# Paged attention in two halves of the heads: one run of 32 tiles instead of two of 16, with the second half's weights prepared in between

## Chip, cores, metric

One core of one Trainium2 chip. The metric is the device time of one execution in microseconds (us), the median of the runs. All times in this text are of that core.

## What is computed

`x` is (64, 32, 512) in fp32. First a quantised linear layer with a low-rank part is added to it, then an attention layer:

```python
x = x + _L0_cond_ref(x, weight, scale_log, codebook, lora_A, lora_B)   # x @ w_eff.T
# attention: B, S, HID = 64, 32, 512; D, HQ, HK = 128, 32, 8; 64 pages of 32 keys, 16 pages a batch
q = rope(rmsnorm(x @ Wq.T, q_norm_w)); k = rope(rmsnorm(x @ Wk.T, k_norm_w)); v = x @ Wv.T
kc, vc = k_cache[block_table], v_cache[block_table]            # 512 old keys a batch
probs = softmax(where(valid, q @ concat(kc, k).T / sqrt(D), -1e30))    # 4 query heads a key head
x = x + (probs @ concat(vc, v)) @ Wo.T
```

## The kernel before, in words

fp32 products are made of three fp16 products (high x high, high x low, low x high), so every operand lies in SBUF as a high and a low part, and most of the data that is turned or loaded is split by ScalarE (high) and VectorE (low).

The setup, once: constants and the effective weight of the first layer (a loop over 63 thresholds: VectorE L554 compares, ScalarE L470 and L471 make diagonals, TensorE L437 sums), while the key pages are turned and split and written to DRAM (`keys_transposed`) and the value pages are split (ScalarE L466, GpSimd L621) and written too. GpSimd starts this stage with the page numbers (L608 to L610: cast, clamp, cast), from which it makes the row numbers of the value gathers (`rows`, L616) and the positions (L617), which VectorE needs for the angles of the rope table (L510). Then `x + layer 1` is made and written transposed to DRAM in 16 tiles of 128 rows (`x1_transposed`).

The heads are done in two halves (4 key heads, 16 query heads), since the weights of one half fill SBUF: `Wt` (projections, six groups of 512 columns: K, four of Q, V) and `WoT` (output, four groups). `with nc.Fori(0, HALVES)` runs three blocks for each half, with a barrier and a clearing of the semaphores after each:

- `tile_block(..., prep=True)`: the weights of this half are loaded to a stage of 1 MB (`load_stage`), turned by TensorE (`turn_weights`, L1052, 40 pieces of four fp32 transposes), split by ScalarE L1157 and VectorE L1268 into `Wt` and `WoT`; in between runs the projection of tile 0.
- `tile_block(..., attn=True)`: 16 tiles of 4 batches. A tile has 16 slots, one for each pair of batch and key head (a unit). In slot s every engine runs, in an order written out by hand: scores of unit s (TensorE L964, L967; VectorE `maxima` L1209; ScalarE `exps` L1110), the turning of the probabilities of unit s - 2 (TensorE L975, ScalarE `probs_high` L1104, VectorE `probs_low` L1214), the values of unit s - 3 (TensorE L998, L1000) and the results of unit s - 4 (ScalarE L1119, VectorE L1227). `TILE_PLAN` spreads over the slots of a tile the projection for the next tile (TensorE L1018, norm on ScalarE and GpSimd, rotation on VectorE L1247 and L1248 at slots 3, 5, 8, 10, 12, turning through the PSUM bank `TRp`, L1028) and the output projection of the tile before (L1039, 48 matmuls in nine parts). Tile 15 has no projection, tile 0 no output projection. After the last slot the pipeline is flushed.
- `tile_block(..., wo=[0])`: the output projection of the last tile, with the first two weight loads for the next half.

SP's queue goes batch by batch: when the maxima of a batch are done, the mask for two batches on, when its scores are done, the 16 pages of keys for three batches on (three buffers); behind these the other loads of the tile, by the place b of the batch in its tile: y (b 0), the new values to DRAM (b 1) and back (b 2), xT for three tiles on (b 2), the rope table for three tiles on and the store of y (b 3). xT and the rope table have two buffers each. The values of a batch are gathered by GpSimd's indirect DMAs (L767), four of 128 rows a batch, one batch ahead, on a queue of their own.

## Time and profile before

| | before |
|---|---|
| median of 3 runs | 2333.78 us (2333.56 to 2333.95) |
| profiled execution | 2333.03 us |
| its span, first to last instruction | 2331.4 us |
| TensorE matmul busy | 2190.5 us, 94% |
| VectorE, ScalarE, GpSimd busy | 1745.9 (75%), 1472.9 (63%), 1245.9 us (53%) |
| mean granted TensorE clock | 0.978 |
| data moved | 419.55 MB, mean 180 GB/s |

The mean of TensorE's share hides its stages: the setup (to 275 us), the preparation of half 1 (to 335), a run of 16 tiles, the stretch between the halves (from some 1270 to 1363), the second run, and the end. Read it stage by stage.

### The profile page before, as it was taken

How to read it: one execution, taken by the hardware profiler on the slowest of the kernel's cores; microseconds unless marked ns; L12 is line 12 of the kernel's file. 1: busy time of each engine (PE TensorE's matmuls, PEld its weight loads, DVE VectorE, ACT ScalarE, POOL GpSimd, SP SyncE). 2: the span in 40 equal slices, each digit the busy share in tenths (PEclk: the TensorE clock that was granted, in tenths of full speed). 3: DMA queues.
4: the chain of work that ended last, by engine and by line, in shares of the span. 5: the costliest groups of instructions: out<-in, count | busy, mean ns of one | idle time of the engine just before them, and what ended most of it. 6: DMA issues, size and time to landing. Idle time of an engine off the chain costs nothing. (4 is left out here: it accounts for less than half of the span.)

```text
span 2331.4 us, 61112 instructions
## 1 busy us (share of the span) xinstructions
PE 2190.5 (94%) x18068; PEld 1425.2 (61%) x18068; DVE 1745.9 (75%) x3942; ACT 1472.9 (63%) x4968; POOL 1245.9 (53%) x2066
## 2 busy tenths in 40 slices
PE   5886789999999999999998789999999999999997
PEld 2443456666666666666665456666666666666664
DVE  6995468777777777777777377777777777777774
ACT  2542367676666666676765466667677666666663
POOL 4330036666666666666664146666666666666562
PEclk9997889999999999999999899999999999999999
DMA  2785666566666666566654665666566666666563
GB/s 100 241 297 161 220 203 178 175 177 177 183 176 185 181 177 180 177 179 178 174 174 130 204 184 171 182 178 177 177 178 180 184 184 179 178 179 177 169 185 108
DMA packets 445186, 419.55 MB, mean 180 GB/s; under 512 B 51615, under 2 KB 371437, under 8 KB 444846
## 3 DMA queue, kind: packets, MB, share of 16 engines
q1 hardware_dynamic: 399726, 277.08, 40.5%
q0 software_dynamic: 40960, 134.25, 19.1%
q10 hardware_dynamic: 4160, 4.19, 0.5%
q8 instruction: 152, 2.49, 0.4%
q14 instruction: 188, 1.54, 0.2%
HBM read 369.12 MB, written 46.21 MB: 178 GB/s over the span
## 5 line engine op out<-in xcount | busy, mean ns | idle before, releaser
L767 POOL DMA_INDIRECT pages<-values_split,rows_s x512 | 516.8, 1009 | 133.3 <-issue 119.8
L1018 PE MATMUL PR<-Wt,xT 128*128 128x512 f16 x2304 | 559.6, 381 | 3.7 <-DVE Wt L1268 3.7
L1104 ACT ACTIVATE pts<-PTp 128x512 f16<-128x512 f32 x512 | 306.7, 599 | 341.4 <-PE PTp L975 277.4
L998 PEld LDWEIGHTS Op<-pts,pages 128*128 128x128 f16 x6144 | 383.3, 98 | 137.6 <-DVE OT L1227 19.3
L998 PE MATMUL Op<-pts,pages 128*128 128x128 f16 x6144 | 427.3, 219 | 17.5 <-DVE OT L1227 12.1
L964 PE MATMUL Sp<-pages,qT 128*128 128x512 f16 x1536 | 417.0, 380 | 7.1 <-PEq L178 6.6
L1110 ACT ACTIVATE masked<-masked,small 128x544 f32<-128x544 f32 x512 | 380.4, 743 | 58.8 <-DVE small L1209 43.7
L1214 DVE TENSOR_TENSOR pts<-PTp,pts 128x512 f16<-128x512 f32 x512 | 351.8, 687 | 86.9 <-ACT pts L1104 50.8
L1209 DVE CUSTOM_DVE_ANT_0 masked<-Sp,mask 128x544 f32<-128x544 f32 x512 | 369.9, 722 | 51.2 <-PE Sp L967 30.8
L1039 PE MATMUL WOp<-WoT,OT 128*128 128x512 f16 x1536 | 379.7, 382 | 9.8 <-PEq L178 9.8
L1018 PEld LDWEIGHTS PR<-Wt,xT 128*128 128x128 f16 x2304 | 225.9, 98 | 200.1 <-issue 9.9
L1227 DVE TENSOR_TENSOR OT<-Op,OT 128x128 f16<-128x128 f32 x512 | 148.3, 290 | 240.2 <-ACT p L1098 153.6
L975 PE MATMUL PTp<-ident,masked 128*128 128x128 f32 x2048 | 325.4, 282 | 1.9 <-DVE pts L1214 1.8
L1220 DVE TENSOR_SCALAR masked<-masked,small 128x544 f32<-128x544 f32 x512 | 291.8, 570 | 18.1
L1325 POOL CAST n<-masked 128x64 f16<-128x64 f32 x512 | 122.0, 238 | 337.8 <-DVE masked L1220 201.5
L1119 ACT ACTIVATE OT<-Op 128x128 f16<-128x128 f32 x512 | 143.6, 281 | 189.3 <-PE Op L980 152.8
L1039 PEld LDWEIGHTS WOp<-WoT,OT 128*128 128x128 f16 x1536 | 146.0, 98 | 131.8 <-issue 15.3
L975 PEld LDWEIGHTS PTp<-ident,masked 128*128 128x128 f32 x2048 | 214.5, 140 | 2.7 <-issue 2.3
L1318 POOL TENSOR_TENSOR qr<-qr,rs_ 128x512 f32<-128x512 f32 x160 | 203.0, 1269 | 6.5 <-DVE rs_ L1248 6.5
L964 PEld LDWEIGHTS Sp<-pages,qT 128*128 128x128 f16 x1536 | 140.1, 98 | 100.9 <-issue 10.6
L1313 POOL TENSOR_TENSOR small<-small 128x4 f32<-128x4 f32 x160 | 184.4, 1153 | 13.3
L967 PEld LDWEIGHTS Sp<-kTn,qT 128*128 128x128 f16 x1536 | 113.8, 97 | 121.8 <-issue 1.7
(196 smaller groups left out, 3070.8 us busy)
## 6 DMA issues: line engine op xcount, KB each, us to landing
pages<-keys_transposed SPq DMA_DIRECT2D x2048, 64.0 KB
mask<-mask_rows SPq DMA_DIRECT2D x128, 128.0 KB
v<-new_values SPq DMA_DIRECT2D x96, 128.0 KB
pages<-in_L_cond_Wq SPq DMA_DIRECT2D x9, 1024.0 KB, 7.3
keys_transposed<-pages SPq DMA_DIRECT2D x32, 256.0 KB, 3.0
values_split<-pages SPq DMA_DIRECT2D x16, 512.0 KB, 3.5
xT<-x_transposed SPq DMA_DIRECT2D x32, 256.0 KB
pages<-values_split,rows_s POOLq DMA_INDIRECT x512
```

What stands on the lines that cost most here:

```text
L767: nc.gpsimd.indirect_dma_start(out=vS[:, n % 2, c, :, :].rearrange("p l n -> p (l n)"), out_offset=None, in_=v_d, in_offset=bass.IndirectO ...
L964: nc.tensor.matmul(Sp[:, 512:1024].rearrange("p (a n) -> p a n", a=NPP), qT[:, tt, ql, q0:q0 + P], kT[n % KBUFS][:, :, h, kl, :], start=(k ...
L975: m = nc.tensor.transpose(PTp[:, c * P:(c + 1) * P], masked[:, u % 3, S + c * P:S + (c + 1) * P], ident[:, :])
L998: nc.tensor.matmul(o, vS[:, par, c, low, h * D:(h + 1) * D], pts[:, u % 2, part, c * P:(c + 1) * P], start=(k == 0), stop=False)
L1018: m = nc.tensor.matmul(bank(k), xb[:, c, xl, :], Wp[:, c, wl, GROUP_COL[k]:GROUP_COL[k] + HID], start=(i == 0), stop=(i == NPASS - 1))
L1039: m = nc.tensor.matmul(WOp[:, :], OT[:, 1 - tt, hq, ol, :], WoT[:, hq, wl, :], start=(hq == 0 and ol == 0 and wl == 0), stop=(hq == QHH - ...
L1104: nc.scalar.activation(pts[:, u % 2, 0, :], PTp[:, :], ACT.Copy).then_inc(G.pt_hi, 1)
L1110: nc.scalar.activation(masked[:, u % 3, :], masked[:, u % 3, :], ACT.Exp, bias=nmax[u % 2], scale=-1.0, accum_out=psum_row[u % 2]).then_in ...
L1209: V.tensor_tensor_reduce(out=masked[:, u % 3, :], in0=Sp[:, 512 - S:1024], in1=mask[:, par, :], scale=-SCALE, scalar=BIG, op0=ALU.add, op1 ...
L1214: V.tensor_tensor(pts[:, u % 2, 1, :], PTp[:, :], pts[:, u % 2, 0, :], ALU.subtract).then_inc(G.pt_lo, 1)
L1220: V.tensor_scalar(masked[:, u % 3, :], masked[:, u % 3, :], rinv[u % 2], None, ALU.mult).then_inc(G.norm_done, 1)
L1318: nc.gpsimd.tensor_tensor(qr[:, m_ % 2, :], qr[:, m_ % 2, :], rs_[:, :], ALU.add).then_inc(G.rope_done, 1)
```

## The change

The loop over the halves is gone. The preparation block runs once, for half 1; then one attention block runs 32 tiles (`ALL_TILES`). Tile 15 now has the projection for tile 16, and tile 16 the output projection of tile 15; the output projection of tile 31 is done by key head inside the flush. Half 2's weights are made in 40 pieces: `load_piece` brings 128 columns of a group (512 B a row) to `wsrc` (two buffers), `turn_piece` turns them through `TRp` at the end of slots 1, 8 and 13 of tiles 0 to 13 (without the first and the last of these 42), ScalarE and VectorE split them into `wdst` one slot later, and `store_piece` writes them to DRAM. The six projection groups are loaded to `Wt` in tile 14, each once its last use there is done, and the four output groups to `WoT` in tile 16. To make room, xT and the rope table have one buffer instead of two, `squares` writes its unused result to `qn` (`sq` is gone), and the copy `rows_s` of the row numbers is gone. GpSimd makes a second list of page numbers, raised by 64, in the setup, with three more instructions.

```diff
+PIECES = (GROUPS + KVH) * 4
+PIECE_SLOTS = [UPT * t + sl for t in range(TILES - 2) for sl in (1, 8, 13)][1:PIECES + 1]
...
                 link(Q.tensor_scalar(btf, btf, float(PAGES - 1), 0.0, ALU.min, ALU.max))
                 Q.tensor_copy(bt_raw, btf).then_inc(G.pages_bounded, 1)
                 g.wait_ge(G.pages_bounded, 1)
+                link(Q.tensor_scalar(btf, btf, 1.0, float(PAGES), ALU.mult, ALU.add))
+                Q.tensor_copy(bt_next, btf).then_inc(G.pages_bounded, 1)
+                g.wait_ge(G.pages_bounded, 2)
+                link(Q.tensor_scalar(btf, btf, 1.0, -float(PAGES), ALU.mult, ALU.add))
...
+        def load_piece(sp, p):
+            s, j = divmod(p, 4)
+            sp.dma_start(wsrc[:, p % 2, :].rearrange("p (c n) -> p c n", c=4), weight_source(1, s)[:, :, j * P:(j + 1) * P]).then_inc(wsrc_loaded[p % 2], 16)
+        def store_piece(sp, p):
+            sp.dma_start(wd_d[p // 4, :, p % 4, :], wdst[:, :, :].rearrange("p l n -> p (l n)")).then_inc(G.w_stored, 16)
...
@@ SP, prep block
                         sp.wait_ge(v5_loaded[0], 3 * 16)
+                        sp.wait_ge(G.proj_done, GROUPS)
+                        load_xT(sp, 1)
+                        sp.wait_ge(G.xT_loaded, 32)
@@ SP, attention block, past = batch - KBUFS, ti, b = divmod(past, BPT)
                             if past >= 0:
                                 sp.wait_ge(G.max_done, KVH * (past + 1))
                                 load_mask(sp, past + 2)
+                                while pieces < PIECES and PIECE_SLOTS[pieces] + 2 <= KVH * (past + 1):
+                                    sp.wait_ge(G.w_lo, pieces + 1)
+                                    store_piece(sp, pieces)
+                                    if pieces + 2 < PIECES:
+                                        load_piece(sp, pieces + 2)
+                                    pieces += 1
+                                if b == 2 and ti + 2 < NT:
+                                    sp.wait_ge(G.proj_done, GROUPS * (ti + 1))
+                                    load_xT(sp, ti + 2)
                                 sp.wait_ge(G.qk_done, KVH * (past + 1))
-                            load_pages(sp, half, numbers, batch % KBUFS)
+                            if batch < NB:
+                                load_pages(sp, numbers, batch % KBUFS)
...
                             if b == 3:
-                                if ti + 3 < TILES:
+                                if ti + 2 < NT:
                                     sp.wait_ge(G.rope_part, len(NORMED) * (ti + 1))
-                                    load_table(sp, ti + 3)
+                                    load_table(sp, ti + 2)
                                 if ti in wo:
                                     store_y(wo.index(ti))
+                            if ti == TILES - 2:
+                                sp.wait_ge(G.w_stored, 16 * PIECES)
+                                for k in ((0, 1), (2, 3), (4, 5), ())[b]:
+                                    sp.wait_ge(G.proj_done, GROUPS * ti + k + 1)
+                                    load_group(sp, k)
+                            if ti == TILES:
+                                for g, parts in (((), (), ((0, 4),), ((1, 6), (2, 7), (3, 9)))[b]):
+                                    sp.wait_ge(G.wo_part, NWO * wo.index(ti) + parts)
+                                    load_output_group(sp, g)
...
@@ TensorE
+                    def turn_piece(p):
+                        turns = turns_before(PIECE_SLOTS[p])
+                        pe.wait_ge(wsrc_loaded[p % 2], 16 * (p // 2 + 1))
+                        if turns:
+                            pe.wait_ge(G.tr_lo, turns)
+                        if p >= 1:
+                            pe.wait_ge(G.w_lo, p)
+                        for c in range(4):
+                            m = nc.tensor.transpose(TRp[:, c * P:(c + 1) * P], wsrc[:, p % 2, c * P:(c + 1) * P], ident[:, :])
+                        m.then_inc(G.w_turned, 1)
...
                         for s in range(NU, NU + FLUSH - 1):
                             if s - 2 < NU:
                                 turn_probs(s - 2)
+                            if s > NU:
+                                group = s - NU - 1
+                                output(NT, tts[0], 4 * group, 4 * group + 4, NU - KVH + 1 + group)
                             values(s - 3)
                             if s - 2 < NU:
                                 turn_new(s - 2)
+                        for group in (2, 3):
+                            output(NT, tts[0], 4 * group, 4 * group + 4, NU - KVH + 1 + group)
@@ ScalarE
+                    def piece_high(p):
+                        a.wait_ge(G.w_turned, p + 1)
+                        if p >= 1:
+                            a.wait_ge(G.w_stored, 16 * p)
+                        nc.scalar.activation(wdst[:, 0, :], TRp[:, :], ACT.Copy, scale=WS).then_inc(G.w_hi, 1)
...
                             rotated_high(ti, tt, plan["turned"][sl])
+                        if s - 1 in piece_at:
+                            piece_high(piece_at[s - 1])
                         if attn:
                             if s >= 2:
                                 probs_high(s - 2)
@@ VectorE
+                    def piece_low(p):
+                        v.wait_ge(G.w_hi, p + 1)
+                        V.scalar_tensor_tensor(wdst[:, 1, :], TRp[:, :], WS, wdst[:, 0, :], ALU.mult, ALU.subtract).then_inc(G.w_lo, 1)
...
                                 new_values_low(ti, tt)
+                        if s - 1 in piece_at:
+                            piece_low(piece_at[s - 1])
                         if sl == 0 and ti - 1 in wo:
                             residual(ti - 1)
                         if attn and s >= 2:
                             probs_low(s - 2)
...
-        with nc.Fori(0, HALVES) as half:
-            tile_block(half, [1], proj=[0], prep=True)
-            tile_block(half, [t % 2 for t in range(TILES)], attn=True, proj=range(TILES - 1), wo=range(1, TILES))
-            tile_block(half, [0], wo=[0])
+        tile_block([1], proj=[0], prep=True)
+        tile_block([t % 2 for t in range(ALL_TILES)], attn=True, proj=range(ALL_TILES - 1), wo=range(1, ALL_TILES + 1))
```

## Rows read from the trace of the kernel before

**Rows 1.** Windows: start:end us, length, busy PE PEld DVE ACT POOL, clock, DMA share, GB/s.

```profile
449.61:509.39 59.78, 59.78 (x526) 39.70 (x525) 46.51 (x113) 41.82 (x148) 36.84 (x64) 1.00 0.62 180
1226.77:1270.48 43.71, 40.83 (x404) 27.85 (x403) 33.51 (x91) 26.66 (x77) 21.70 (x46) 1.00 0.54 159
1270.48:1363.99 93.51, 63.79 (x381) 43.06 (x379) 41.89 (x70) 40.92 (x120) 17.86 (x24) 0.87 0.55 174
1363.99:1419.49 55.50, 49.85 (x428) 32.31 (x427) 44.16 (x107) 38.71 (x139) 35.11 (x62) 0.96 0.66 186
1419.49:1479.84 60.35, 60.35 (x526) 40.18 (x525) 46.18 (x111) 41.34 (x146) 36.20 (x62) 0.99 0.57 167
```

**Rows 2.** Timeline of PE, tiles 1 and 15, last slot: start us, us, line, out<-in.

```profile
389.83 0.23 PE L967 MATMUL Sp<-kTn,qT 128*128 128x32 f16 x3
...
1226.77 0.23 PE L967 MATMUL Sp<-kTn,qT 128*128 128x32 f16 x3
...
2300.75 0.20 PE L967 MATMUL Sp<-kTn,qT 128*128 128x32 f16 x2
```

**Rows 3.** Timeline of PE in the preparation of half 2, transposes back to back.

```profile
1333.77 0.60 PE L1028 MATMUL TRp<-ident,qr 128*128 128x128 f32 x4
1334.21 0.60 PE L1052 MATMUL Op<-ident,pages 128*128 128x128 f32 x4
```

**Rows 4.** Timeline of ACT, DVE and PE in tile 14, slots 9, 13 and 14.

```profile
1201.33 0.60 ACT L1104 ACTIVATE pts<-PTp 128x512 f16<-128x512 f32 x1 [0.49 <-PE PTp L975]
...
1202.04 0.69 DVE L1214 TENSOR_TENSOR pts<-PTp,pts 128x512 f16<-128x512 f32 x1
1203.03 0.17 DVE L1218 RECIPROCAL small<-small 128x1 f32<-128x1 f32 x1 [0.31 <-ACT masked L1110]
...
1217.99 0.69 DVE L1254 TENSOR_TENSOR qT<-TRp,qT 128x512 f16<-128x512 f32 x1
...
1219.14 0.81 PE L964 MATMUL Sp<-pages,qT 128*128 128x512 f16 x3
```

**Rows 5.** Timeline of SP's queue and DVE around a tile's start; DMA issues with landing.

```profile
994.52 0.43 SPq L807 DMA_DIRECT2D rope_s<-rope_table  x1
...
1000.75 0.68 DVE L1247 TENSOR_TENSOR qr<-qn,rope_s 128x512 f32<-128x512 f32 x1
...
1041.31 0.43 SPq L804 DMA_DIRECT2D xT<-x_transposed  x1
...
pages<-in_x SPq DMA_DIRECT2D x16, 256.0 KB, 2.9
```

**Rows 6.** Timeline of POOL and PE: last gather for a batch, its first use.

```profile
1067.07 0.99 POOL L767 DMA_INDIRECT pages<-values_split,rows_s  x1 [0.16 <-issue]
...
1075.02 0.67 PE L998 MATMUL Op<-pts,pages 128*128 128x128 f16 x9
```

**Rows 7.** Timeline of POOL, DVE and ACT in the setup.

```profile
40.34 1.91 POOL L610 CAST WoT<-WoT 128x1024 int32<-128x1024 f32 x1
42.36 3.35 POOL L616 TENSOR_SCALAR rows<-WoT 32x256 uint32<-32x256 f32 x2
...
54.29 1.22 DVE L510 TENSOR_TENSOR WoT<-WoT 128x1024 f32<-128x1024 f32 x1 [5.17 <-POOL WoT L617]
55.43 3.14 DVE L554 TENSOR_SCALAR qT<-Wt,WoT 128x2048 f16<-128x2048 f32 x1
...
60.67 1.06 ACT L466 ACTIVATE pages<-v 128x1024 f16<-128x1024 f32 x1 [14.76 <-DMA values_split<-pages]
```

**Rows 8.** Timeline of PE and DVE: nine output matmuls, the flush, the end.

```profile
1216.41 2.11 PE L1039 MATMUL WOp<-WoT,OT 128*128 128x512 f16 x9
1218.35 0.83 PE L998 MATMUL Op<-pts,pages 128*128 128x128 f16 x12
...
2304.53 0.84 PE L998 MATMUL Op<-pts,pages 128*128 128x128 f16 x12 [0.55 <-DVE OT L1227]
...
2326.84 0.69 DVE L1264 SCALAR_TENSOR_TENSOR y<-WOp,y 128x512 f32<-128x512 f32 x1 [16.27 <-PE WOp L1039]
```

More of the change, by code:

```diff
@@ L62 @@
 NCB = 64
+ALL_TILES = HALVES * TILES
 ROUND = 1.5 * 2.0 ** 23
@@ L413, in _ @@
                 sp.wait_ge(G.mask_stored, 16)
[L414 removed]
+                sp.wait_ge(G.pages_stored, 32)
             @block.tensor
@@ L652, in build @@
         x1b = [qn[:, 0, :], qn[:, 1, :]]
-        xTb = [xT[:, i, :, :, :] for i in range(2)]
+        xTb = [pages[:, 4096 + 1024 * i:5120 + 1024 * i].rearrange("p (c l n) -> p c l n", c=IC, l=2) for i in range(2)]
         TPS = TILES
@@ L831, in tile_block, with pieces_before, turns_before @@
             slots = [(s, tts[s // UPT], s % UPT) for s in range(UPT * NT)]
+            NWO = len(plan["wo"])
+            piece_at = {g: p for p, g in enumerate(PIECE_SLOTS)} if attn else {}
+            def pieces_before(slot):
+                return sum(g < slot for g in piece_at)
+            def turns_before(slot):
+                return sum(UPT * t + sl < slot for t in proj for sl in plan["turn"])
             def unit(u):
@@ L875, in _ @@
                             sp.wait_ge(G.pe_done, 4 * (s - 1))
-                            load_stage(sp, half, s)
-                            load_pages(sp, half, numbers, n, range(4 * a_, 4 * a_ + 4))
+                            load_stage(sp, 0, s)
+                            load_pages(sp, numbers, n, range(4 * a_, 4 * a_ + 4))
                         load_numbers(sp, 0)
@@ L933, in _ @@
+                        load_y(len(wo) - 1)
                         store_y(len(wo) - 1)
-                        for par in range(2):
-                            sp.wait_ge(xT_loaded[par], 16 * (TILES // 2 - 1))
-                    elif wo:
-                        load_y(0)
-                        load_stage(sp, (half + 1) % HALVES, 0)
-                        load_stage(sp, (half + 1) % HALVES, 1)
-                        store_y(0)
-                        for done in stage_loaded:
-                            sp.wait_ge(done, 16)
```

153 lines of the change are left out of this document (80 added, 73 removed).

## Prediction

> **What bounds the kernel now.** I read the windows of one tile first, then the stretch between the two halves, then the waits inside a tile, and last the setup. In a tile of the steady run (16 units of scores, softmax and values, called slots here) TensorE is busy for 59.78 of 59.78 us at clock 1.00, with VectorE at 46.5, ScalarE at 41.8 and GpSimd at 36.8 us [rows 1]. So inside the attention run only what TensorE itself executes counts. The period is the same everywhere: the last scores matmuls (L967) of slot 0 start at 389.83 in tile 1 and at 1226.77 in tile 15, 836.94 us for 14 tiles, 59.78 us each [rows 2]. The exception is the seam between the halves. From the last scores of half 1 to the first of half 2 there pass 93.51 us, in which TensorE works 63.79 us at a granted clock of 0.87 [rows 1]: the flush of the pipeline, a block of its own for the last output projection, a barrier, the 40 weight pieces of half 2 with its first projection, another barrier. The tiles on both sides are not full either: the last one has no projection, the first no output, and the second of half 2 takes 60.35 us.
>
> **The seam is replaced by three full tiles.** From the start of tile 15 (1226.77) to the start of the third tile of half 2 (1479.84) there are 43.71 + 93.51 + 55.50 + 60.35 = 253.07 us [rows 1]. Afterwards the same stretch holds tiles 15, 16 and 17, each with a projection (for the next tile) and an output projection (of the one before): the last projection of half 1, which was absent, is now that of half 2's first tile; the output block of 48 matmuls goes into tile 16. All three carry the mix of a steady tile, so I take 3 x 59.78 = 179.34 us. Difference: -73.7 us. It contains the flush, two barriers, the first output block, the idle time and the low clock at once, so I do not count them again.
>
> **Pieces in the tiles of half 1.** 40 pieces, each four fp32 transposes on TensorE, one ScalarE and one VectorE instruction of 512 columns. Two such groups of four start 0.44 us apart when TensorE runs without a gap [rows 3], so 40 x 0.44 = +17.6 us, all on the path, since TensorE has no idle time in these tiles to hide them. The ScalarE and VectorE halves are hidden if a slot has room. In slot 9, which takes the piece of slot 8, VectorE's subtraction of the probabilities (L1214) at 1202.04 is followed by 0.31 us idle before the next reciprocal, ScalarE is idle 0.49 us before the probabilities' copy, and everything that waits for TensorE moves back by the 0.44 us of the transposes. VectorE's extra instruction costs some 0.6 us of its time (L1214 takes 0.69, its followers start 0.60 after it), against 0.31 + 0.44 = 0.75 us. ScalarE has 0.49 + 0.44 = 0.93 for its 0.50 to 0.60 [rows 4]. Hidden, barely; slots 2 and 14 are lighter, as no rotation stands ahead of them. Behind the piece's instruction on VectorE stand L1214 and the normalisation, for which TensorE waits one slot later. The piece of slot 13 uses the bank TRp, which the copy that started at 1217.99 (0.69 us) leaves 0.46 us before slot 14 began at 1219.14 [rows 4]: also free in time. Low bound of the 40 pieces: 17.6 (the matmuls must run). High bound: each piece's two instructions in series uncovered, 40 x (0.60 + 0.69) more, 69 us in all. I take 17.6, as TensorE never waited in the steady tiles for engines that are 22% or more idle [rows 1].
>
> **SP's queue.** Each piece adds a store and a load, about 0.45 us of issue each, ahead of the 16 page loads, and the piece reads and writes 256 KB each way. Two buffers become one. xT for the next tile was issued at 1041.31, behind pages and values; it is now issued ahead of the pages of the same event, about 10 us earlier, and is needed at the next tile's start (about 1047): no cost. The rope table keeps its place behind the pages: issued at 994.52, and since its buffer is now single it is needed in the same tile, where the first rotation ran at 1000.75 [rows 5]. That leaves 6.2 us, less 0.9 for the piece's two issues: 5.3 us. A 256 KB load took 2.9 us in the setup [rows 5]. Cost zero; if it lands late VectorE stalls in slot 3 of each tile. The page loads are two batches (30 us) ahead, so their shift is free.
>
> **Weights by group.** Six loads of 1 MB in tile 14 (two behind each of three batches) and four in tile 16. The last piece is in tile 13, so the wait for all stores is met. Each load waits for a projection finished at least one slot before, the last of the four output groups for the end of slot 15; behind that wait stand the next batch's mask and pages, which have 15 and 30 us. Traffic is 180 GB/s at a DMA share of 0.62 in a steady tile [rows 1], so the queues saturate near 290. 2 MB more per batch of four slots (59.78 / 4 = 14.9 us) is 134 GB/s more, 314 in all, for three batches: some 1.1 MB or 4 us of backlog. The third case is 3 MB issued together, some 13 us of backlog at 290 less the gathers. The mask behind it has 15 us and the value gather, a queue of its own, was issued at 1067.07 and first used at 1075.02, 8 us [rows 6]. I take 0; bounds 0 and 20 us.
> The Trainium skill, "DMA: Bandwidth & Descriptors", section "Queues, rings and completion order", says that an engine takes its queues in turn but that a completion mark lands only after all earlier writes of that engine, across queues, which speaks against this edit: a gather's completion could wait for the bulk loads. By it the result would be the rival "burst" below; no trace here shows it.
>
> **Setup.** GpSimd gets three more 128x1024 instructions for the second half's page numbers, placed ahead of the row numbers and positions. This is on the path. VectorE's L510 sits idle 5.17 us until GpSimd's L617 is done, and ScalarE's values copy at 60.67 waits 14.76 us for a store which waits for GpSimd's next work [rows 7]. Afterwards VectorE is almost without a gap for the rest of that stage, so nothing gives the delay back. One such instruction starts 2.02 us after the one before [rows 7]: 3 x 2.0 = +6.0 us; bounds 0 (all regained later) and 10.
> VectorE's threshold instruction took 3.14 us at 55.43, while GpSimd subtracted values, where L510 before it took 1.22 [rows 7]. The Trainium skill, "SBUF — State Buffer", section "Who interferes with whom", says that such a VectorE mode and GpSimd lock one another out for a whole instruction; by it the three new instructions could each wait for one threshold instruction, some 3 x 1.2 = 3.6 us more, 9.6 in all, an estimate. GpSimd's L610 took 1.91 us in the very stretch in which VectorE compares thresholds, so I keep 6.0.
>
> **Preparation and end.** The preparation block now ends with the load of xT(1), waited for behind the values' load; one fewer load stands at its head. +0.5 us (-1 to +3). At the end the last output is woven into the flush. Before, 30.65 us passed from the last scores (2300.75) to the end (2331.4) [rows 2, 8]. The third last values start at 2304.53, then the flush's own work is 2.9 us and the 48 matmuls 48 x 0.216 = 10.4 (nine of them from 1216.41 to 1218.35 [rows 8]), plus 0.7 us for the transposes that now wait for the residual: last matmul about 2318.4, VectorE 0.7, and 3.87 us from VectorE's end at 2327.53 to the end of the span stay: 2323.0. -8.4 us (-11 to -4; the store and reload of y take some 6 us and lie beside the matmuls).
>
> **Sum.** -73.7 + 17.6 + 6.0 + 0.5 - 8.4 = -58.0 us. Span 2331.4 - 58.0 = 2273.4 us. The profiled execution took 2333.03, 1.63 above its span, and the median of the runs 0.75 above that: 2273.4 + 1.63 + 0.75 = 2275.8 us, 2.5% faster.
>
> **Rivals.**
> Pieces not covered: VectorE's order puts the piece ahead of L1214, and slot 9 had only 0.15 us to spare by the count above. If half of 1.29 us per piece comes through, 40 x 0.65 = +26 us: 2302 us; all of it, 2327. For it: VectorE holds slots 8 to 10 with 22% idle at best. Against: not one TensorE wait in steady tiles. 0.08.
> Burst: mask, pages or gathers late behind the 3 MB and 6 MB: +5 to +20 us once, 2281 to 2296. 0.12.
> Setup delay regained: GpSimd's later values copies wait for ScalarE, so the pipe has room; 2270, and down to 2266 if the seam's tiles are a little short as well. 0.10.
> Table late, the slower case: one mechanism, at one place, slot 3 of 31 tiles. It costs 31 us for each us that the table lands late beyond what VectorE's idle time absorbs. At 58 / 31 = 1.9 us it takes all, that is, from a landing of 5.3 + 1.9 = 7.2 us after the issue on; at 8 us the time would be about 2360 including no absorption. Measured is 2.9 us with empty queues; between pages it isn't shown. 0.04.
> The seam does not close (the projection of tile 15 or the output of tile 17 waits for weights, as the loads chain behind SP's waits): 40 to 60 us back, 2316 to 2336. 0.02.
> Forecast: 0.64.
>
> **How the numbers follow.** Forecast, setup regained and burst make 0.86; range 2265 to 2296. Faster by over 0.2% (about what a measurement of this kernel can tell from no change, 4.7 us): 0.95; within: 0.01; slower: 0.04.
>
> **What would show it.** TensorE busy near 100% in every slice from tile 1 to tile 31; tiles with three pieces 59.78 + 1.32 = 61.1 us, others 59.78; no drop at the middle; L510 in the setup near 60.3 instead of 54.3; 22 us after the last scores. A tile near 62 or more, or idle time of TensorE ended by VectorE, shows pieces not covered; VectorE idle at its first rotation of a tile shows a late table; a gap in tile 14 or 17 ended by a DMA shows the burst. A second price for the transposes, or a tile 15 that isn't 59.78, would make the sum wrong.

## The result, and the profile after

| | before | after |
|---|---|---|
| median | 2333.8 us (2333.56 to 2333.95) | 2269.14 us (2267.21 to 2271.64, 4 runs) |
| ratio to before | | 0.9727, 95% interval 0.9712 to 0.9741 |
| profiled execution | 2333.03 us | 2268.09 us |
| its span | 2331.4 us | 2266.1 us |
| TensorE matmul busy | 2190.5 us, 94% | 2165.7 us, 96% |
| mean granted clock | 0.978 | 0.985 |
| data moved | 419.55 MB | 438.32 MB |

The change saves 2.7%; the forecast was 2275.8 us, 2.5%. The forecast's span was 2273.4 us and the measured one is 2266.1 us, so the forecast left out 7.3 us of gain. The page of the changed kernel first, in 40 slices of 57 us: TensorE's row, the clock and the DMA.

```profile
PE   5786779999999999999999999999999999999998
PEclk9997889999999999999999999999999999999999
DMA  3784666667667666666768768666666666566663
```

TensorE is at 9 from the first full tile to the last; the drop at the middle is gone. Now the windows of the stretches that the sum was made of: a tile with three pieces, tile 13 (two pieces), tile 14 (no piece, but the six group loads), then tiles 15, 16 and 17, which stand where the seam was, and tile 18. Columns as in [rows 1].

```profile
460.00:521.10 61.10, 61.10 (x538) 41.06 (x537) 47.86 (x117) 43.03 (x149) 36.54 (x64) 1.00 0.69 200
1123.79:1184.45 60.66, 60.66 (x533) 40.61 (x532) 47.29 (x115) 42.76 (x149) 36.50 (x64) 1.00 0.65 193
1184.45:1244.23 59.78, 59.78 (x525) 39.71 (x524) 46.52 (x113) 41.63 (x147) 37.26 (x63) 1.00 0.82 252
1244.23:1304.02 59.79, 59.79 (x526) 39.72 (x524) 46.36 (x113) 41.67 (x147) 36.56 (x64) 1.00 0.72 212
1304.02:1363.80 59.78, 59.78 (x525) 39.71 (x524) 46.62 (x113) 41.32 (x147) 36.56 (x63) 1.00 0.63 193
1363.80:1423.58 59.78, 59.78 (x525) 39.70 (x524) 46.18 (x113) 41.75 (x147) 36.60 (x64) 1.00 0.76 237
1423.58:1483.36 59.78, 59.78 (x525) 39.74 (x524) 46.66 (x113) 41.61 (x147) 36.54 (x64) 1.00 0.61 179
```

Each window is as long as TensorE's work in it, at clock 1.00. Three pieces make 61.10, two make 60.66, tile 14 and the three tiles of the seam 59.78 each, as the steady tile in [rows 1]. From tile 1 to the last scores TensorE waited for anybody for 2.7 us in all, and all eight of these waits lie in tile 31, which has no projection (engine, line, waited for: us, times, longest):

```profile
PE Op L1037 <- DVE OT L1298: 2.4, 7, 0.4
PE PTp L1014 <- DVE pts L1285: 0.3, 1, 0.3
```

The setup, timeline of GpSimd and VectorE, answering [rows 7]. GpSimd's three added instructions are L620, L621 and L623; VectorE's L518 is L510 of before.

```profile
43.21 1.91 POOL L620 TENSOR_SCALAR WoT<-WoT 128x1024 f32<-128x1024 f32 x1
45.18 1.91 POOL L621 CAST pages<-WoT 128x1024 int32<-128x1024 f32 x1
47.17 1.90 POOL L623 TENSOR_SCALAR WoT<-WoT 128x1024 f32<-128x1024 f32 x1
49.18 1.53 POOL L628 TENSOR_SCALAR rows<-WoT 32x256 uint32<-32x256 f32 x2
...
57.33 1.23 DVE L518 TENSOR_TENSOR WoT<-WoT 128x1024 f32<-128x1024 f32 x1 [9.16 <-POOL WoT L629]
```

They take 5.9 us, as forecast, but L518 starts 3.04 us later than L510 did, not 6. The last scores of slot 0 of tile 0 start at 337.75, against 336.72 before: of the 6.5 us forecast for setup and preparation, 1.0 is left in this pair of traces. The preparation block itself went from 61.3 to 60.6 us (275.40 to 336.72 before, 277.14 to 337.75 after). Last the rope table in tile 14 (SyncE's issue, VectorE's first use) and the end of the program, answering [rows 5, 8]:

```profile
1191.70 0.43 SPq L818 DMA_DIRECT2D rope_s<-rope_table  x1
...
1197.56 0.68 DVE L1318 TENSOR_TENSOR qr<-qn,rope_s 128x512 f32<-128x512 f32 x1
```

```profile
2244.25 0.23 PE L1006 MATMUL Sp<-kTn,qT 128*128 128x32 f16 x3
...
2256.47 5.34 PE L1095 MATMUL WOp<-WoT,OT 128*128 128x512 f16 x24
...
2261.85 0.69 DVE L1335 SCALAR_TENSOR_TENSOR y<-WOp,y 128x512 f32<-128x512 f32 x1 [4.58 <-PE WOp L1095]
```

From the last scores to the end there are 2266.1 - 2244.25 = 21.85 us, before 30.65.

### The profile page after: what moved, and what is told of

It reads as the page before. It is cut to its first block, busy times and chain, and to the rows that moved or that the text cites. A ratio compares the mean times of both kernels' runs of the same rounds, so it can differ in the third digit from the quotient of the medians.

```text
span 2266.1 us, 61278 instructions
## 1 busy us (share of the span) xinstructions
PE 2165.7 (96%) x18068; PEld 1417.1 (63%) x18068; DVE 1728.6 (76%) x3942; ACT 1470.7 (65%) x4967; POOL 1242.9 (55%) x2067
## 2 busy tenths in 40 slices
DMA packets 472535, 438.32 MB, mean 193 GB/s; under 512 B 52861, under 2 KB 399308, under 8 KB 471694
## 4 chain that ended last, share of the span: by engine, by line
PE 83%; DVE 1%; issue 0%; ACT 0%; another core or an unknown queue 0%; DVEq 0%; ACTq 0%
PE PR L1058 21%; PE Op L1037 15%; PE WOp L1095 15%; PE Sp L1003 14%; PE PTp L1014 11%; PE TRp L1071 3%; PE Sp L1006 2%; PE Op L1019 1%; PE Op L1039 1%; PE TRp L1082 1%; DVE masked L1280 0%; DVE pts L1285 0%; DVE OT L1298 0%; DVE y L1335 0%; DVE masked L1291 0%
## 5 line engine op out<-in xcount | busy, mean ns | idle before, releaser
L778 POOL DMA_INDIRECT pages<-values_split,rows x512 | 516.0, 1008 | 194.4 <-issue 181.4
L1291 DVE TENSOR_SCALAR masked<-masked,small 128x544 f32<-128x544 f32 x512 | 281.3, 549 | 18.1
```

What stands on the lines that cost most here:

```text
L778: nc.gpsimd.indirect_dma_start(out=vS[:, n % 2, c, :, :].rearrange("p l n -> p (l n)"), out_offset=None, in_=v_d, in_offset=bass.IndirectO ...
L1291: V.tensor_scalar(masked[:, u % 3, :], masked[:, u % 3, :], rinv[u % 2], None, ALU.mult).then_inc(G.norm_done, 1)
```

## The experiments

All are edits of the changed kernel, but for one, which is an edit of the kernel before. The runs that give an interval were timed beside the kernel before, which on that chip had a median of 2332.07 us (2332.04 beside the last version) with single runs from 2326.5 to 2337.1, so 2 to 3 us of a single run mean nothing. Where a time stands without an interval, it is one run, and the reading rests on its trace.

### The same kernel again

No edit.

> The changed kernel once more, to see which part of its span differs between executions (its four runs lie between 2267.2 and 2271.6 us). Theory A: the tiles repeat to 0.02 us (61.10 and 59.78), and what differs lies ahead of tile 0, in the setup with its DMA waits. Rival: tiles with group loads or pieces differ, by 1 us or more.

Measured: 2269.46 us (2267.45 to 2270.66, 5 runs), ratio 0.9731 (0.9715 to 0.9747). Tiles with pieces are 61.10 again, and L518 started at 57.01. But tile 14 took 60.48 and tile 15 60.70 us in this execution (59.78 both in the first), the two tiles in and behind which the group loads run: 1.6 us, as the rival had it. What held them, timelines of TensorE and VectorE:

```profile
1243.52 0.83 PE L1037 MATMUL Op<-pts,pages 128*128 128x128 f16 x12 [0.54 <-issue]
...
1259.92 0.69 DVE L1318 TENSOR_TENSOR qr<-qn,rope_s 128x512 f32<-128x512 f32 x1 [1.79 <-DMA rope_s<-rope_table]
...
1262.09 0.84 PE L1037 MATMUL Op<-pts,pages 128*128 128x128 f16 x12 [0.74 <-DVE OT L1298]
```

The first is the first matmul on the values gathered for the last batch of tile 14. The results of VectorE and ScalarE that it needs were done by 1241.0, 2.5 us earlier, so of what the kernel makes it wait for, the landing of the gather is left; the profile names no cause. The second is the rope table of tile 15, late by 1.8 us, of which TensorE felt 0.7.

The setup varies more. Nine traces here have the changed kernel's setup as it stands (the first, this one and the seven runs below from the doubled transposes to the tail); in them the first scores start between 334.3 and 339.1 us, with a median of 337.9.

### Setup: where GpSimd's three instructions stand

```diff
-                link(Q.tensor_scalar(btf, btf, 1.0, float(PAGES), ALU.mult, ALU.add))
-                Q.tensor_copy(bt_next, btf).then_inc(G.pages_bounded, 1)
-                g.wait_ge(G.pages_bounded, 2)
-                link(Q.tensor_scalar(btf, btf, 1.0, -float(PAGES), ALU.mult, ALU.add))
...
+                late = pages3[:, 2 * B * NPP:4 * B * NPP].bitcast(F32)
+                link(Q.tensor_copy(late, bt_raw))
+                link(Q.tensor_scalar(late, late, 1.0, float(PAGES), ALU.mult, ALU.add))
+                Q.tensor_copy(bt_next, late).then_inc(G.pages_bounded, 1)
```

> The three GpSimd instructions for the second half's page numbers stand behind the value copies of the setup instead of ahead of the row numbers. The forecast's step (they delay everything by 6.0 us) expects 6 us less than the changed kernel, 2263. Theory A (they delay VectorE's first angle instruction by 3.0 us, since GpSimd's row and position instructions run at full speed once VectorE has run out of threshold work, and one to two of these reach tile 0): that instruction at 54.3 instead of 57.3, GpSimd's first row numbers again 3.4 us for two, 1 to 2 us less in all. Rival B (all is regained): no difference.

Measured: 2267.74 us (2264.15 to 2268.93), ratio 0.9723 (0.9706 to 0.974). The first scores are at 337.07 us, as they were. L518 did start earlier:

```profile
54.50 1.23 DVE L518 TENSOR_TENSOR WoT<-WoT 128x1024 f32<-128x1024 f32 x1 [6.41 <-POOL WoT L625]
```

Of the 2.8 us gained there 0.8 are left where the first matmul on x starts, 202.2 us against 203.0 (202.4 to 204.0 in the nine traces). The forecast's 6 us are refuted: the median is 1.4 and 1.7 us below the changed kernel's two, and the single runs overlap, so this does not tell it from nothing.

The other way round, the kernel before with the three instructions added at the same place:

```diff
+                link(Q.tensor_scalar(btf, btf, 1.0, float(PAGES), ALU.mult, ALU.add))
+                Q.tensor_copy(bt_next, btf).then_inc(G.pages_bounded, 1)
+                g.wait_ge(G.pages_bounded, 2)
+                link(Q.tensor_scalar(btf, btf, 1.0, -float(PAGES), ALU.mult, ALU.add))
```

> The kernel before with those three GpSimd instructions alone, at the place where the change puts them. Forecast's step: +6.0 us, 2339.8. Theory A: VectorE's first angle instruction at 57.3 instead of 54.3, +1 to +2 us in all, about 2335. Rival B: no difference, 2333.8.

Measured: 2334.36 us (2329.19 to 2339.42) beside 2332.07, ratio 1.0009 (0.9999 to 1.002): +2.3 us, at the edge of what can be told, and 4.7 at most by the interval, under the forecast's 6. VectorE's instruction again starts only 2.75 us later than in [rows 7]:

```profile
57.04 1.23 DVE L511 TENSOR_TENSOR WoT<-WoT 128x1024 f32<-128x1024 f32 x1 [8.00 <-POOL WoT L622]
```

In this pair of traces the first matmul on x starts 2.6 us later (203.4 against 200.8) and the first scores 1.2 us later (337.9 against 336.7). So part of the 3 us is lost again before tile 0, but the place where it is lost differs from pair to pair.

### Setup: positions first

The positions, for which alone VectorE waits, are made first; the page numbers and row numbers get a buffer of their own and are made in parts behind the first value subtractions.

```diff
-                btf = ang
+                btf = pages3[:, 2 * B * NPP:4 * B * NPP].bitcast(F32)
...
+                def row_numbers(q):
+                def page_numbers_part(c):
...
+                    if 1 <= c <= 5:
+                        g.wait_ge(G.v_lo, c + 1)
+                        page_numbers_part(c)
```

> The changed kernel with the positions as GpSimd's first instructions of the setup's second stage, the value copies next, and page and row numbers cut into parts that stand behind value copies 1 to 5 (in a buffer of their own, since the angles overwrite the old one). If VectorE's work bounds that stage, the 9.2 us wait for the positions and the 3.6 us wait that follows from the late value copies go: 10 to 13 us less than the changed kernel, about 2257. Rival: the stage is bound by the stores and loads of the pages (ScalarE waited 50.7 us for stores of values), then only 2 to 4 us go.

Measured: 2262.02 us (2256.18 to 2262.84), ratio 0.9691 (0.9673 to 0.9709), some 7 us below the changed kernel: between the two expectations. VectorE's wait is gone entirely. The first scores start at 332.4 us, below all nine traces of the changed setup. What it gives is less than the wait's 9.16 us: both engines now work at once again and their instructions grow (timeline of VectorE, groups of GpSimd by line: busy us, mean ns, idle):

```profile
51.15 3.15 DVE L518 TENSOR_TENSOR WoT<-WoT 128x1024 f32<-128x1024 f32 x1
...
L625 POOL TENSOR_SCALAR rows<-pages,WoT 32x256 uint32<-32x256 f32 x8 | 16.6, 2074 | 0.8
```

In the changed kernel the same two are 1.23 us and, in the mean of the eight row-number instructions, 0.71 us:

```profile
L628 POOL TENSOR_SCALAR rows<-WoT 32x256 uint32<-32x256 f32 x8 | 5.7, 709 | 0.8
```

So the wait of VectorE is one side of a trade: while it waits, GpSimd's row numbers take 0.71 us each, and 2.07 when it does not. VectorE's 3.15 us are a wait too: it started 0.9 us behind GpSimd's values subtraction (50.24 to 53.22) and ended 1.1 us after it. Its 1.23 us in the changed kernel are with a start 0.05 us ahead of GpSimd's next one, which then took 3.15 us, where the shortest of its form takes 2.1.

### The pieces: TensorE's half doubled

```diff
-                        for c in range(4):
+                        for c in (0, 1, 2, 3, 0, 1, 2, 3):
```

> Each of the 40 pieces is turned twice (eight fp32 transposes instead of four, same result). Theory A (TensorE alone sets the tile's period): tiles with three pieces go from 61.10 to 62.42 us, the whole by +16 to +18 us, 2286. Rival (a period is set by the chain of ScalarE and VectorE, and transposes hide in it): less than half of that.

Measured: 2285.0 us, span 2283.0. The tile at 460 us:

```profile
460.00:522.40 62.40, 62.40 (x552) 42.35 (x550) 47.82 (x116) 43.33 (x150) 36.60 (x63) 1.00 0.66 196
```

Another 1.3 us for three pieces, 0.44 for each four transposes, again with no idle time. TensorE's work alone sets the period.

### The pieces: the split doubled and tripled

ScalarE's and VectorE's instruction for each piece, once more (range(1)) or twice more (range(2)), with the same operands:

```diff
+                        for again in range(1):
+                            repeats[0] += 1
+                            nc.scalar.activation(wdst[:, 0, :], TRp[:, :], ACT.Copy, scale=WS).then_inc(G.chain_a, 1)
+                            a.wait_ge(G.chain_a, repeats[0])
...
+                        for again in range(1):
+                            repeats[0] += 1
+                            V.scalar_tensor_tensor(wdst[:, 1, :], TRp[:, :], WS, wdst[:, 0, :], ALU.mult, ALU.subtract).then_inc(G.chain_v, 1)
+                            v.wait_ge(G.chain_v, repeats[0])
```

> The ScalarE and the VectorE instruction of each piece run twice, each first one waited for by its own engine before the second (some 0.6 and 0.7 us more on each engine and piece). The forecast's count says slot 9 had 0.15 us to spare, so about 0.45 us or more of each of the 13 pieces of slot 8 should come through: tiles near 61.6 to 62. Theory A (there is more room, since TensorE's waits lie two slots behind): tiles stay at 61.10 us.

> The same instructions three times (1.2 to 1.5 us more on each engine and piece). Forecast's count: over 1 us for each piece of slot 8 and something for the others, tiles at 62.5 to 64 us. Theory A with a room of one to two us: tiles between 61.1 and 62.5 us.

Measured, doubled: 2269.86 us, span 2267.9. Tripled: 2298.49 us, span 2296.4. A tile of each:

```profile
460.00:521.10 61.10, 61.10 (x540) 41.05 (x537) 49.92 (x119) 45.05 (x154) 36.63 (x63) 1.00 0.68 200
```

```profile
500.00:563.10 63.10, 61.53 (x537) 41.19 (x536) 52.30 (x123) 46.55 (x156) 36.81 (x63) 1.00 0.67 199
```

Doubled, VectorE is 2.06 us busier in a tile and the tile is not 0.01 us longer. The forecast's "0.15 us to spare" would have let some 0.5 us of the piece of slot 8 through, by the expectation 61.6 us or more. Tripled, a tile is 63.08 us, +1.98, or 0.66 for each piece. Of the 1.48 us by which VectorE is busier for each piece, 0.66 came through, so some 0.8 us of its time was free there beside the piece's own instruction, by both runs at least 0.7. These are means. By slot, slot 10 is 0.3 us longer (4.03 against 3.72), slot 3 0.5 and slot 14 1.1: the piece of slot 8, for which the forecast had counted 0.15 us, had 1.1 to 1.2 us of room, and the piece of slot 13 is the tight one. Where the cover ended, waits of TensorE from 500 to 1000 us:

```profile
PE TRp L1071 <- DVE wdst L1349: 7.7, 8, 1.1
PE PTp L1014 <- DVE pts L1291: 4.4, 15, 0.4
```

Once a tile the turned queries of slot 14 wait for the bank TRp, which the piece of slot 13 still holds; the other two pieces hold up the low part of the probabilities, one wait each at slots 3 and 10.

### The burst: six group loads at once

```diff
-                                for k in ((0, 1), (2, 3), (4, 5), ())[b]:
+                                for k in ((), (), (0, 1, 2, 3, 4, 5), ())[b]:
```

> All six projection groups of half 2 (6 MB) are loaded behind the third batch of tile 14 instead of two behind each of three batches. The forecast's count for the burst: queues saturate near 290 GB/s, less some 70 for the gathers, so 6 MB take some 27 us; the next mask stands behind them and has 15 us, so tile 14 or 15 is longer by 8 to 15 us. Rival (bulk loads leave room, or the mask's wait is not reached): tile 15 at 59.8 to 61 us. By a rule that gathers complete only behind the bulk loads, TensorE would also wait for gathered values in tile 14.

Measured: 2283.19 us, span 2281.2. Tile 15 takes 74.68 us, 14.9 more than 59.78, and every other tile is as before. SyncE's queue, then what VectorE and TensorE waited for from 1244 to 1300 us, then windows of 10 us:

```profile
1238.39 15.67 SPq L828 DMA_DIRECT2D Wt<-weights_split  x6
1255.12 2.92 SPq L805 DMA_DIRECT2D mask<-mask_rows  x1
1258.24 9.09 SPq L797 DMA_DIRECT2D pages<-keys_transposed  x16
1267.39 0.42 SPq L818 DMA_DIRECT2D rope_s<-rope_table  x1
```

```profile
DVE qr L1318 <- DMA rope_s<-rope_table: 11.8, 1, 11.8
...
PE Op L1037 <- DVE OT L1298: 10.8, 1, 10.8
PE PR L1058 <- DMA Wt<-weights_split: 0.9, 1, 0.9
```

```profile
1245.00:1255.00 10.00, 9.15 (x73) 5.60 (x73) 6.55 (x17) 6.11 (x22) 4.04 (x8) 1.00 1.08 363
1255.00:1265.00 10.00, 6.80 (x62) 4.31 (x59) 2.26 (x6) 4.77 (x20) 3.76 (x6) 1.00 1.08 347
1265.00:1275.00 10.00, 2.40 (x17) 1.85 (x18) 4.02 (x10) 1.78 (x7) 2.34 (x4) 0.50 0.62 185
```

A burst does bite, but neither through the mask nor through a gather, the two that the forecast looked at. The six issues hold SyncE's own queue for 15.67 us, with the mask, the pages and the single-buffered rope table behind them. The first two take 0.6 us each, as in the changed kernel, the other four 3.2 to 4.2. The table comes 11.8 us late. TensorE waits 10.8 us for it and 0.9 for a weight group, and then runs at a granted clock of 0.50, its lower level of 1.2 GHz: its work in this tile takes 63.03 us instead of 59.78, which makes up the rest of the 14.9. No wait for gathered values shows: the last gather for tile 15's first batch starts at 1249.48, when five of the six loads are issued and the third has not landed (1253.9), and its values are needed 8.3 us after it.

### The rope table: when it lands, and what a late one costs

SyncE waits for the table right behind its load, so that its next instruction marks the landing:

```diff
                                     load_table(sp, ti + 2)
+                                    sp.wait_ge(G.table_loaded, 16 * (ti + 2))
```

> The changed kernel, but SyncE waits for the rope table right behind its load, so that the start of its next instruction marks the table's landing. In the changed kernel's trace the table of one tile is issued at 1191.7 and first used at 1197.56, 5.9 us later. The forecast took 2.9 us for the landing (a 256 KB load in the setup): SyncE would go on 2.9 to 3.4 us after the issue, and 2.5 us of room are left; time unchanged, 2269 (2266 to 2273). The rival 'table late' puts the landing nearer to 5 us and over, as 16 page loads are in the queues ahead of it: SyncE would go on 4.5 to 6 us after the issue, with under 1.4 us of room; time still unchanged, since only SyncE's y store waits. Either would be wrong if the table were over 5.9 us: then VectorE would show waits at its rotation.

Measured: 2268.77 us. From the load's issue to SyncE's next instruction there are 2.92 us in the median of the tiles (2.60 to 4.36). The tile at 522 us:

```profile
522.35 0.43 SPq L818 DMA_DIRECT2D rope_s<-rope_table  x1
525.10 0.35 SPq L894 DMA_DIRECT2D out_y<-y  x1
```

The forecast's 2.9 us, taken from a load in the setup, holds in the tiles too, with 5.9 us available in tile 14. Read in the changed kernel for tiles 1 to 30, from the issue to VectorE's first use, the room is 4.3 to 6.7 us but for two tiles: in tile 1 the first use came 2.7 us after the issue, with a wait of 0.7 us (1.2 here), and in tile 15 3.4 us after it, with a wait of 0.2. TensorE felt neither in the changed kernel's first trace; the repeat, where the wait in tile 15 was 1.8 us, shows that there was little to spare.

Then the table is issued late on purpose, behind the maxima of slot 3 of the tile that needs it:

```diff
+                                    if ti + 1 < NT:
+                                        sp.wait_ge(G.max_done, UPT * (ti + 1) + 4)
                                     load_table(sp, ti + 2)
```

> The changed kernel, but SyncE issues the rope table only once VectorE's maxima of slot 3 of the tile that needs it are done, about 1196.8 instead of 1191.7 in the traced tile, 0.8 us ahead of the first rotation. With a landing of 3 us the rotation waits 2.2 us, with 5 us 4.2 us, in each of about 30 tiles. The prediction's rival says that it costs 31 us for each us beyond what VectorE's idle time absorbs. Theory A (VectorE's idle of some 1.3 us in a slot absorbs little, since the wait stands ahead of the reciprocal and the normalisation that TensorE needs one slot later): half to all of the lateness comes through, +35 to +120 us. Rival B (TensorE reads VectorE's results one slot of 3.7 us later, and a wait of 2 to 4 us is regained within two or three slots as slots 4 to 6 are light): under 15 us in all, tiles of 59.8 to 60.2 us.

Measured: 2363.08 us, span 2361.1, slower than the kernel before. Tiles take 62.0 to 65.8 us. What VectorE and TensorE waited for in all tiles, and three tiles in a row:

```profile
DVE qr L1320 <- DMA rope_s<-rope_table: 98.9, 30, 3.9
...
PE Op L1039 <- DVE OT L1300: 69.8, 37, 2.9
```

```profile
1281.10:1343.06 61.96, 59.96 (x526) 39.66 (x525) 46.09 (x114) 41.58 (x146) 36.59 (x64) 1.00 0.69 209
1343.06:1405.36 62.30, 59.95 (x526) 39.63 (x525) 46.05 (x114) 41.56 (x146) 36.55 (x64) 1.00 0.57 171
1405.36:1469.34 63.98, 61.61 (x526) 40.33 (x525) 46.67 (x114) 41.62 (x146) 36.54 (x64) 0.97 0.73 233
```

VectorE waits 3.3 us a tile. About 1.0 of it is absorbed: TensorE waits 2.0, 2.3 and 2.4 us in these three tiles, where VectorE waited 3.0, 3.4 and 3.4. But the third tile pays 1.66 us more, since its clock falls: after TensorE's 2.4 us of waiting the granted clock is 0.50 from 1432 to 1434 us, 0.60 and 0.69 in the windows of 1 us on either side:

```profile
1431.00:1432.00 1.00, 1.00 (x13) 0.72 (x10) 0.89 (x3) 0.68 (x2) 1.00 (x1) 0.60 0.98 410
1432.00:1433.00 1.00, 1.00 (x4) 0.43 (x3) 0.67 (x2) 1.00 (x6) 0.83 (x2) 0.50 1.06 451
```

Of tiles 1 to 30, 15 have such a stretch, each at a mean clock of 0.97 and some 1.65 us dearer, and 15 have none. The length of the wait alone does not part them: it was 2.0 to 2.9 us in the first and 0.8 to 2.6 us in the others.

The setup of this execution was 3.4 us shorter (first scores at 334.31), so the cost is taken from the first scores to the last: 2004.95 us against 1906.50, +98.5. TensorE stood idle 66.9 us more (73.5 against 6.7), the low clock of the 15 tiles makes 24.6, and 7.0 are spread in small parts that weren't taken apart. Rival B, that a wait of 2 to 4 us is regained in light slots, is refuted.

### The tail: no output group woven into the flush

```diff
-                            if s > NU:
-                                group = s - NU - 1
-                                output(NT, tts[0], 4 * group, 4 * group + 4, NU - KVH + 1 + group)
...
-                        for group in (2, 3):
+                        for group in range(4):
```

> The changed kernel, but all four groups of the last tile's output matmuls run after the flush instead of two of them woven into it. The tail (from the last scores to the end) took 21.9 us, where the kernel before took 30.7. If the weaving fills TensorE's waits in the flush (the forecast's view: 48 matmuls beside 2.9 us of the flush's own work), the waits come back: +2 to +3 us in the tail, 24 to 25. If the rest of the 8.8 us comes from the separate block and its barrier, the tail stays well under 30. The rival, that the weaving is all of the gain: tail at 29 to 31 us, time 2277 or more.

Measured: 2269.07 us; the tail is 2267.1 - 2243.89 = 23.2 us, 1.4 more than 21.85. TensorE's waits in it:

```profile
PE Op L1037 <- DVE OT L1295: 1.5, 2, 1.0
PE PTp L1014 <- DVE pts L1282: 0.3, 1, 0.3
```

With the weaving the first is 0.5 us alone, and the second 0.3. So the weaving gives 1.4 us of the 8.8, a little less than expected, and the other 7.4 us came with the block of its own. The 48 output matmuls in the kernel before, then in this run:

```profile
2314.24 12.56 PE L1039 MATMUL WOp<-WoT,OT 128*128 128x512 f16 x48 [4.91 <-PEq L178]
```

```profile
2252.30 10.52 PE L1095 MATMUL WOp<-WoT,OT 128*128 128x512 f16 x48
```

Before, TensorE stands idle 4.91 us ahead of them, waiting for its own queue, and then does them at a granted clock of 0.50 for the first 4 us (0.83 in the mean), which takes 2.0 us more than the same 48 at clock 1.00. Together they are 6.95 of the 7.4 us. The rival, that all of the gain is the weaving, is refuted.

### The best version

Positions first, and in the preparation the load of x for tile 1 issued ahead:

```diff
+                        sp.wait_ge(G.proj_done, GROUPS)
+                        load_xT(sp, 1)
...
-                        sp.wait_ge(G.proj_done, GROUPS)
-                        load_xT(sp, 1)
```

> The version with the row numbers made in parts behind the value copies (2262.0 when run alone), with the load of x for tile 1 issued before the first groups of projections instead of behind them in the preparation block. The preparation's wait for it was read as 0.1 us, so this should repeat the earlier version: 2262 us (2256 to 2264), ratio 0.969, first scores at 332 us. The rival, that the earlier run's gain of 7 us was scatter of the setup stage (the kernel before alone scatters by 5 us), gives 2267 to 2270 and first scores at 336 to 338.

Measured: 2260.54 us (2258.15 to 2262.45, 5 runs), ratio 0.9697 (0.9682 to 0.9711). It repeats positions first, and the intervals of both lie below that of the changed kernel run again (0.9715 to 0.9747). The rival, that the gain was scatter of the setup, is refuted: the first scores start at 328.1 us here, at 334.3 or later in the nine traces. Moving x gave nothing: the preparation took 61.05 us, with positions first alone 60.99. This version is 0.4% faster than the changed kernel and 3.1% faster than the one before.

## Why the prediction was right, and where it was not

**The seam (-73.7).** Right to 0.1 us. Tiles 15, 16 and 17 run from 1244.23 to 1423.58, 179.35 us against the 179.34 forecast (0.9 us longer in the repeat, where the table was late in tile 15). Taking the whole stretch between two marks and filling it with full tiles avoided pricing the flush, barriers and low clock one by one.

**The pieces (+17.6).** TensorE's price of 0.44 us a piece is exact: 1.32 in 12 tiles, 0.88 in tile 13, and the doubled transposes show that nothing else takes part. Tile 0 with its two pieces took 52.79 us, against 53.11 before, so they seem to have cost nothing in its unfilled start. But that tile took 52.3 to 54.4 us in the four other traces without an edit to it or its pieces, so this isn't shown. Together +16.4, a term over-priced by 1.2 in this pair of traces. The step that failed is the cover, "hidden, barely": slack was counted between two neighbouring instructions of one slot (0.15 us), but TensorE needs those results a slot later, and VectorE can run behind until then. The doubled split shows that 0.7 us more fits, the tripled one that slot 8's piece has over 1 us of room. So the rival "pieces not covered" was given a chance it didn't have at this size, though its mechanism is real: it is what the tripled split shows.

**Setup and preparation (+6.5).** The step that failed: "VectorE is almost without a gap for the rest of that stage, so nothing gives the delay back", a term mis-sized as 6.5 where the pair of traces has 1.0 and the three instructions alone cost 2.3 in the medians of the kernel before (4.7 at most). The instructions cost 5.9 us on GpSimd as counted. Half came back at once: the row and position instructions behind them took 1.53 us a pair and 0.34 us, where before the first took 3.35 [rows 7], as VectorE had by then run out of work and stood idle (9.16 us instead of 5.17). Part of the rest was gone by the first scores: L518 was 2.8 and 2.75 us apart in the two experiments, the first scores 0.7 and 1.2. Which instructions give this back wasn't isolated, and the scatter of these stages (4.8 us over nine traces) is larger.
The Trainium skill, "SBUF — State Buffer", section "Who interferes with whom", says that GpSimd's port pair is shared with VectorE and that the one that comes second is blocked for a whole instruction. The rows agree with it (VectorE's L518 takes 1.23 us where it starts first and 3.15 where it starts behind GpSimd, GpSimd's row numbers 0.71 and 2.07), but the estimate that the forecast drew from it had the wrong sign. It said 9.6 us instead of 6.0, since it charged the lock to the added instructions; these took 1.9 us each, as their like before, and the delay left the row numbers behind them without VectorE beside them.

**SyncE's queue (0).** Right in the traced execution: the landing was taken as 2.9 us and the room as 5.3; measured are 2.92 (up to 4.4) and 4.3 to 6.7, but 2.7 and 3.4 in tiles 1 and 15. Tile 15 is a place where the zero is by luck: the room was taken from a tile without group loads, and in the repeat the table came late there and cost most of 0.9 us. The rival "table late" had the right price too: 31 us for each us of lateness, and 98.9 us of lateness cost 98.5. That it needed no allowance for absorption is a coincidence of two things that the forecast didn't have: 1.1 us a tile is absorbed, and 0.8 us a tile comes back as low clock, with 0.2 in small parts.

**Weights by group (0).** Right for the change as written in the first trace, where the six loads come two by two: no TensorE wait in tile 14, 15 or 16. In the repeat tiles 14 and 15 cost 1.6 us more, so the zero doesn't hold in every execution; the rival "burst" began at 5 us. Two numbers of its working were wrong. The DMA queues do not saturate near 290 GB/s: they moved 363 in the burst. And the victim in the burst isn't the mask or a gather but the rope table behind SyncE's own blocked queue. The size, 5 to 20 us, held in the experiment (14.9).
The Trainium skill, "DMA: Bandwidth & Descriptors", section "Queues, rings and completion order", says that a completion mark lands only after the earlier writes of its engine, across queues. By it the gathers would have come late behind 6 MB. In the experiment built for it no engine waited for a gathered value, so with 8.3 us of lead there this trace does not bear the rule out as a cost; it doesn't refute it either, as the landing of a gather wasn't measured. The lead is not 8 us everywhere, as the forecast took it from [rows 6]: counted from the end of a batch's last gather it is 5.0 to 8.8 us in tiles 1 to 30, and the wait of 0.54 us in the repeat ended 5.9 us after its last gather. That wait would fit the rule, but a like one (0.45 us, the same batch, tile 24) stands in the trace with the page numbers last, where no bulk load runs, so the cause stays open.

**The end (-8.4).** -8.8 measured. 1.4 of it is the weaving, 7.4 the end of the separate block, of which 4.9 are TensorE's idle time and 2.0 the low clock behind it. The forecast modelled only the matmuls' places in the new tail and never priced that block by itself, so it was right in the sum and silent on where the gain is. (Its last matmul, 2304.53 + 2.9 + 10.4 + 0.7, comes at 2318.5, not 2318.4; nothing hangs on that.)

**The sum.** -73.7 + 16.4 + 1.0 - 8.8 = -65.1, against -65.3 measured; the other 0.2 are in tile 31. Of the 7.3 us that the forecast missed, 5.5 are the setup and preparation, 1.2 the first tile, 0.4 the end. The misses all lie on one side, so none hid another. The rival "setup delay regained", put at 2270 and given 0.10, is near what happened in that stage; its mechanism, room in GpSimd's later values copies, wasn't tested.

## What to carry to other kernels

Where one engine is full at clock 1.00, price an edit by that engine's instructions alone and ask of the others only whether they are late by the time it needs them, one slot on: here the 38 pieces outside tile 0 cost exactly their transposes, and the split had room for twice its size. A delay in front of an engine that shares something with the one it waits for is not added whole: look at what the waiting engine stops disturbing. When a queue gets bulk loads, look first at what is behind them on the same issuing engine and has the shortest lead, above all a buffer that has just become single.

## What the runs showed of the hardware that wasn't expected

- GpSimd and VectorE slow some of each other's instructions by a factor of 2.5 to 3 in the setup: one of GpSimd (32x256, fp32 to integers) takes 0.71 us with VectorE idle and 2.07 with it busy, VectorE's 128x1024 fp32 product 1.23 where it starts 0.05 us ahead of GpSimd's and 3.15 where it starts 0.9 us behind. Not all grow: GpSimd's 128x1024 ones took 1.9 us beside VectorE's threshold work.
- With one wait of TensorE of 0.8 to 2.9 us in each of 30 tiles, 15 of these waits were followed by a stretch at a granted clock of 0.50, which cost 1.65 us more, the shortest of them 2.0 us long; 15 were not, the longest of them 2.6 us. At the end of the kernel before, 4.9 us of idle time were followed by 4 us at 0.50.
- Six 1 MB loads hold SyncE for 15.67 us when they come together, the first two 0.6 us each and the other four 3.2 to 4.2, while two together were issued in 1.32 us. The DMA engines moved 347 to 363 GB/s over 10 us, where the forecast had taken 290 as their limit.
